# Attention and two gated layers on one core: value matmuls of two steps back to back, and both ends of the run in halves

## What is computed

```python
def attn(x, ...):                      # 16 heads of 8 features
    q, k, v = split((x @ w_qkv).reshape(B, S, 16, 24))
    w = relu(q @ k.T / sqrt(8))
    a = (w / (w.sum(-1) + 1e-6)) @ v
    return layernorm(x + a @ w_out + b_out) * gamma + beta

def ffn(x, ...):                       # w1, w2 dequantised from integers
    h = layernorm(x) * ln_gamma + ln_beta
    return x + 0.5 * (silu(h @ w1 + b1) @ w2 + b2)

x = x + 0.5 * ffn(layernorm(x))
x = x + attn(layernorm(x))
x = x + 0.5 * ffn(layernorm(x))
```

## Time and profile before

| | us |
|---|---|
| median of 3 runs | 387.11 (385.79 to 387.66) |
| the profiled execution, in all | 389.17 |
| its span, first to last instruction | 387.4 |
| TensorE busy | 376.3 (97%) |
| VectorE busy | 285.6 (74%) |
| ScalarE busy | 224.9 (58%) |
| GpSimd busy | 219.4 (57%) |

### The profile page before, as it was taken

How to read it: one execution, slowest core, us unless ns; L and a number is a source line. 1 busy time by engine, 2 the same in 40 slices (tenths; PEclk the granted TensorE clock), 3 DMA queues, 4 the chain that set the end, 5 groups by cost and what they waited for, 6 DMA issues and landing times.

```text
span 387.4 us, 11728 instructions
## 1 busy us (share of the span) xinstructions
PE 376.3 (97%) x4614; PEld 195.3 (50%) x4614; DVE 285.6 (74%) x682; ACT 224.9 (58%) x406; POOL 219.4 (57%) x446
## 2 busy tenths in 40 slices
PE   8988999999999999999999999999999999999996
PEld 8863523353564435553454445553564445323685
DVE  3544687889767988688877977787867977876660
ACT  2235556666756577466857577566756675646302
POOL 4685035737891589438982589437973574263052
PEclk9998999999999999999999999999999999989999
DMA  7318101710171006400261006400350016200001
GB/s 141 50 34 186 30 1 43 177 29 3 32 188 57 3 3 145 104 28 2 57 164 58 2 3 151 122 2 2 83 139 30 2 26 148 73 3 2 3 13 45
DMA packets 14967, 23.05 MB, mean 60 GB/s; under 512 B 3136, under 2 KB 4416, under 8 KB 14912
## 3 DMA queue, kind: packets, MB, share of 16 engines
q1 hardware_dynamic: 11520, 17.71, 19.4%
q10 hardware_dynamic: 3392, 4.59, 4.7%
HBM read 3.41 MB, written 2.10 MB: 14 GB/s over the span
## 4 chain that ended last, share of the span: by engine, by line
PE 80%; DVE 6%; DMA 5%; POOL 3%; issue 2%; ACT 1%; SPq 1%; ACTq 0%; POOLq 0%; DVEq 0%
PE o_bank L439 29%; PE scores L424 15%; PE post_bank L369 9%; PE pre_bank L369 8%; PE pre_bank L374 5%; DMA q_op<-q_parts 3%; PE pre_bank L375 3%; DMA b_rows<-in_L_ffn_fc_bias_dram 2%; PE post_bank L374 2%; DVE probs L815 2%; PE pre_bank L362 2%; PE pre_bank L399 2%; PE post_bank L399 2%; PE post_bank L375 2%; PE post_bank L362 1%
## 5 line engine op out<-in xcount | busy, mean ns | idle before, releaser
L815 DVE TENSOR_SCALAR probs<-scores 128x512 f32<-128x512 f32 x256 | 164.0, 682 | 50.5 <-PE scores L424 48.1
L608 ACT ACTIVATE probs<-scores 128x512 f32<-128x512 f32 x256 | 138.6, 595 | 69.4 <-PE scores L424 69.2
L439 PE MATMUL o_bank<-probs,v_op 128*32 128x512 f32 x1024 | 137.9, 611 | 0.0
L424 PE MATMUL scores<-q_op,k_op 32*128 32x512 f32 x512 | 78.4, 498 | 2.6 <-DMA q_op<-q_parts 2.0
L424 PEld LDWEIGHTS scores<-q_op,k_op 32*128 32x128 f32 x512 | 32.0, 183 | 87.9 <-issue 51.6
L439 PEld LDWEIGHTS o_bank<-probs,v_op 128*32 128x32 f32 x1024 | 21.7, 109 | 30.4 <-issue 24.9
L540 ACT ACTIVATE pre_y<-pre_bank,b_sum,s_col 128x512 f32<-128x512 f32 x28 | 21.8, 779 | 25.8 <-PE pre_bank L399 25.8
L844 POOL TENSOR_SCALAR norm_x_var<-norm_x_mv 128x4 f32<-128x4 f32 x24 | 4.7, 196 | 53.1 <-DVE norm_x_mv L678 52.6
L844 POOL TENSOR_SCALAR norm_y_var<-norm_y_mv 128x4 f32<-128x4 f32 x8 | 1.7, 218 | 55.2 <-DVE norm_y_mv L678 55.2
L369 PE MATMUL pre_bank<-w,pre_y 128*32 128x128 f32 x1024 | 32.3, 274 | 0.0
L369 PEld LDWEIGHTS pre_bank<-w,pre_y 128*32 128x32 f32 x1024 | 27.3, 110 | 8.0 <-issue 8.0
(11 more groups left out here) (133 smaller groups left out, 534.6 us busy)
## 6 DMA issues: line engine op xcount, KB each, us to landing
k_op<-k_parts SPq DMA_DIRECT2D x64, 128.0 KB, 2.7
q_op<-q_parts SPq DMA_DIRECT2D x63, 128.0 KB, 2.8
pre_x<-in_L_attn_x_dram ACTq DMA_DIRECT2D x8, 256.0 KB, 2.8
out_dram<-o_rows ACTq DMA_DIRECT2D x8, 256.0 KB, 2.0
w_int<-in_L_ffn_fc_q_dram SPq DMA_DIRECT2D x2, 256.0 KB, 3.9
s_rows<-in_L_ffn_fc_scales_dram SPq DMA_DIRECT2D x1, 256.0 KB, 6.9
w_raw<-in_L_attn_w_qkv_dram SPq DMA_DIRECT2D x1, 192.0 KB, 7.8
wo<-in_L_attn_w_out_dram SPq DMA_DIRECT2D x8, 8.0 KB, 7.4
```

The lines of the kernel that those rows point to most:

```text
L424: mm(scores[i][:, j, :], k_op[rows, g, P * kt:P * (kt + 1)], q_op[rows, g, :], start=True, stop=True).then_inc(scores_done[i], 1)
L439: last = mm(o_bank[pair][VW * j:VW * (j + 1), :], v_op[:, kt, heads_of(g).start + 2 * j, :], probs[:, s % 2, j, :], start=(odd == 0 and kt ...
L608: activation(probs[:, s % 2, j, :], scores[0][:, j, :], ACT.Relu).then_inc(probs_done[0], 1)
L815: v.tensor_scalar(probs[:, s % 2, 2 + j, :], scores[1][:, j, :], 0.0, None, ALU.max).then_inc(probs_done[1], 1)
```

## The change

- Values are issued in even steps only: those of s-2 and s-1, one after the other, behind the scores of s. `probs` gets a third buffer, taken in turn over the whole run (`HELD`), and the evictions wait for the values of three steps ago.
- *pre* of batch 0 and *post* of batch 7 are worked in two halves of 256 tokens (`first.*`, `last.*`, function `edge` on TensorE, ScalarE and VectorE, `half_deviations` on GpSimd). The halves take the banks of both stages and separate semaphores; q and k of batch 0 take score banks, halves of `op` the `pre` bank and `o_bank[0]`. Batch 0's `x` is loaded in two halves by two queues, the last result stored in two.
- Small constants come in two arrays: four columns in one, four rows (b2, gamma, beta, b_out) in another, each loaded by one DMA; the host lays them side by side. `b2_quarter` is made inside the first residual, behind the mix. 
- `alone`, `bank` and the special cases for it are gone. All orders are new.

The core of the diff:

```diff
+HELD = 3
...
 PE_FIRST = [
-    "warm_up.19", "pre.hT", "weights.b1", "warm_up.2", "pre.fc1.0", "pre.fc1.1", "pre.fc1.2", "pre.fc1.3", "pre.fc2.0", "pre.fc2.1",
-    "pre.fc2.2", "pre.fc2.3", "warm_up.15", "pre.uT", "warm_up.3", "pre.k", "pre.q", "pre.v", "warm_up.7", "pre.hT@1", "warm_up.4"
+    "warm_up.14", "weights.b1", "warm_up.2", "first.hT.0", "first.fc1.0.0", "first.fc1.1.0", "first.fc1.2.0", "first.hT.1",
+    "first.fc1.3.0", "first.fc2.0.0", "first.fc1.0.1", "first.fc2.1.0", "first.fc2.2.0", "first.fc2.3.0",
+    "first.fc1.1.1", "first.fc1.2.1", "first.fc1.3.1", "first.fc2.0.1", "first.fc2.1.1", "first.fc2.2.1",
+    "first.fc2.3.1", "warm_up.9", "first.uT.0", "first.k.0", "first.q.0", "first.uT.1", "first.v.0", "first.k.1",
+    "first.q.1", "first.v.1", "warm_up.4", "pre.hT@1", "warm_up.5"
 ]
 PE_ORDER = [
-    ([], ["post.fc2.0@-2", "pre.fc1.0@1"]),
-    (["post.fc2.1@-2", "post.fc2.2@-2", "post.fc2.3@-2", "pre.fc1.1@1"], []),
-    (["post.op@-1", "pre.fc1.2@1"], []),
+    ([], ["post.fc1.3@-2", "pre.fc1.0@1"]),
+    (["post.fc2.0@-2", "pre.fc1.1@1", "post.fc2.1@-2", "post.fc2.2@-2", "post.fc2.3@-2"], []),
+    (["pre.fc1.2@1", "post.op@-1"], []),
     (["pre.fc1.3@1"], []),
-    (["pre.fc2.0@1"], []),
-    ([], ["pre.fc2.1@1"]),
+    ([], []),
+    (["pre.fc2.0@1", "pre.fc2.1@1"], []),
+    ([], []),
     (["pre.fc2.2@1", "pre.fc2.3@1"], []),
     ([], []),
+    (["post.hT@-1"], []),
     ([], []),
-    ([], ["post.hT@-1"]),
-    ([], []),
-    ([], ["pre.uT@1", "post.fc1.0@-1"]),
-    ([], ["pre.k@1", "post.fc1.1@-1"]),
-    ([], ["pre.q@1", "post.fc1.2@-1"]),
+    (["post.fc1.0@-1", "pre.uT@1"], []),
+    ([], ["pre.k@1"]),
+    (["post.fc1.1@-1", "pre.q@1"], []),
     ([], ["pre.v@1"]),
-    (["post.fc1.3@-1", "pre.hT@2"], []),
+    (["post.fc1.2@-1", "pre.hT@2"], []),
 ]
 PE_LAST = ([], [
-    "post.fc2.0@-2", "post.fc2.1@-2", "post.fc2.2@-2", "post.fc2.3@-2", "post.op@-1", "warm_up.32@-1", "post.hT@-1", "warm_up.5@-1",
-    "post.fc1.0@-1", "post.fc1.1@-1", "post.fc1.2@-1", "post.fc1.3@-1", "post.fc2.0@-1", "post.fc2.1@-1",
-    "post.fc2.2@-1", "post.fc2.3@-1"
+    "post.fc1.3@-2", "post.fc2.0@-2", "last.op.0@-1", "last.op.1@-1", "post.fc2.1@-2", "post.fc2.2@-2",
+    "post.fc2.3@-2", "warm_up.26@-1", "last.hT.0@-1", "last.fc1.0.0@-1", "last.fc1.1.0@-1", "last.fc1.2.0@-1", "last.hT.1@-1",
+    "last.fc1.3.0@-1", "last.fc2.0.0@-1", "last.fc1.0.1@-1", "last.fc1.1.1@-1", "last.fc1.2.1@-1",
+    "last.fc1.3.1@-1", "last.fc2.0.1@-1", "last.fc2.1.1@-1", "last.fc2.2.1@-1", "last.fc2.1.0@-1",
+    "last.fc2.2.0@-1", "last.fc2.3.0@-1", "last.fc2.3.1@-1"
 ])
 ACT_FIRST = [
-    "pre.hT", "pre.fc1.0", "pre.fc1.1", "pre.load_x", "pre.fc1.2", "pre.fc1.3", "pre.load_x@1", "pre.uT",
-    "pre.k", "pre.q", "pre.v", "pre.hT@1"
+    "first.hT.0", "first.fc1.0.0", "first.hT.1", "first.fc1.1.0", "first.fc1.2.0", "first.fc1.3.0",
+    "first.fc1.0.1", "pre.load_x@1", "first.fc1.1.1", "first.fc1.2.1", "first.fc1.3.1", "first.uT.0",
+    "first.t_u.0", "first.k.0", "first.q.0", "first.uT.1", "first.t_u.1", "first.k.1", "first.v.0",
+    "first.q.1", "pre.load_x", "first.v.1", "pre.hT@1"
 ]
 ACT_ORDER = [
-    ["pre.fc1.0@1"],
+    ["post.fc1.3@-2", "pre.fc1.0@1"],
     ["pre.fc1.1@1"],
-    ["pre.fc1.2@1", "post.store@-2", "pre.load_x@2"],
+    ["pre.load_x@2", "pre.fc1.2@1"],
     ["pre.fc1.3@1"],
     ["post.y_apply@-1"],
     [],
     [],
     [],
     [],
+    [],
     ["post.hT@-1"],
-    [],
     ["pre.uT@1", "post.fc1.0@-1"],
-    ["pre.k@1", "post.fc1.1@-1"],
-    ["pre.q@1", "post.fc1.2@-1"],
-    ["pre.v@1"],
-    ["pre.hT@2", "post.fc1.3@-1"],
+    ["pre.k@1"],
+    ["pre.q@1"],
+    ["post.fc1.1@-1", "pre.v@1"],
+    ["post.store@-2", "post.fc1.2@-1", "pre.hT@2"],
 ]
 ACT_LAST = [
-    "post.hT@-1", "post.store@-2", "post.fc1.0@-1", "post.fc1.1@-1", "post.fc1.2@-1", "post.fc1.3@-1",
-    "post.store@-1"
+    "post.fc1.3@-2", "last.hT.0@-1", "last.fc1.0.0@-1", "post.store@-2", "last.fc1.1.0@-1", "last.hT.1@-1",
+    "last.fc1.2.0@-1", "last.fc1.3.0@-1", "last.fc1.0.1@-1", "last.fc1.1.1@-1", "last.fc1.2.1@-1",
+    "last.fc1.3.1@-1", "last.store.0@-1", "last.store.1@-1"
 ]
 DVE_FIRST = [
-    "pre.x_stats", "pre.x_apply", "weights.w1", "weights.w1_parts", "pre.hT", "weights.b1", "weights.w2",
-    "weights.w_qkv", "pre.x1", "pre.x1_stats", "pre.x_stats@1", "pre.u_apply", "pre.uT", "pre.k_lo",
-    "pre.q_lo", "pre.hT@1"
+    "first.x_stats.0", "first.x_stats.1", "weights.w1", "first.x_apply.0", "weights.w1_hi", "weights.w1_lo",
+    "weights.b1", "first.hT.0", "first.x_apply.1", "weights.w2", "first.hT.1", "weights.w_qkv", "first.x1.0",
+    "first.x1_stats.0", "first.u_apply.0", "pre.x_stats@1", "first.x1.1", "first.uT.0", "first.x1_stats.1",
+    "first.k_lo.0", "first.u_apply.1", "first.q_lo.0", "first.uT.1", "first.k_lo.1", "first.q_lo.1", "pre.hT@1"
 ]
 DVE_ORDER = [
     ["oT.1@-1", "den.1@-1"],
-    ["a.1@-1", "post.out@-2", "aT@-1"],
+    ["a.1@-1", "aT@-1", "post.out@-2"],
     ["post.y@-1", "post.y_stats@-1"],
     [],
     ["pre.x_stats@2"],
     ["post.x2@-1"],
-    ["post.x2_stats@-1", "pre.x1@1"],
-    [],
+    ["post.x2_stats@-1"],
+    ["pre.x1@1"],
     ["pre.x1_stats@1"],
     [],
     ["post.hT@-1"],
-    [],
-    ["oT.0", "den.0", "pre.k_lo@1"],
+    ["oT.0"],
+    ["den.0", "pre.k_lo@1"],
     ["pre.q_lo@1"],
     ["a.0"],
     ["pre.hT@2"],
 ]
 DVE_LAST = [
-    "oT.1@-1", "den.1@-1", "a.1@-1", "aT@-1", "post.out@-2", "post.y@-1", "post.y_stats@-1", "post.y_apply@-1",
-    "post.x2@-1", "post.x2_stats@-1", "post.x_apply@-1", "post.hT@-1", "post.out@-1"
+    "oT.1@-1", "den.1@-1", "a.1@-1", "aT@-1", "last.y.0@-1", "last.y.1@-1", "last.y_stats.0@-1",
+    "last.y_apply.0@-1", "last.y_stats.1@-1", "last.x2.0@-1", "last.y_apply.1@-1", "last.x2_stats.0@-1",
+    "last.x2.1@-1", "post.out@-2", "last.x_apply.0@-1", "last.x2_stats.1@-1", "last.hT.0@-1",
+    "last.x_apply.1@-1", "last.hT.1@-1", "last.out.0@-1", "last.out.1@-1"
 ]
 POOL_FIRST = [
-    "pre.x_stats", "weights.b2", "pre.xr", "pre.x1_stats", "pre.x_stats@1", "pre.x_apply@1", "pre.xr@1",
-    "v_in.0", "post.u_bias", "pre.uT", "v_in.1", "pre.x1_beta"
+    "first.x_stats.0", "first.x_stats.1", "pre.xr", "first.x1_stats.0", "first.x1_stats.1", "pre.x_stats@1",
+    "pre.x_apply@1", "v_in.0", "pre.xr@1", "pre.x1_beta", "v_in.1", "pre.uT", "post.u_bias"
 ]
 POOL_ORDER = [
     [],
     [],
-    ["post.y_stats@-1", "post.y_gamma@-1"],
-    [],
-    ["v_in.2", "post.x2_stats@-1", "post.x_apply@-1", "pre.x1_stats@1"],
-    [],
+    [],
+    [],
+    ["v_in.2", "v_in.3", "post.y_gamma@-1", "pre.x_stats@2"],
+    [],
+    ["post.x2_stats@-1", "post.x_apply@-1"],
+    [],
+    ["pre.x1_stats@1"],
     ["pre.u_apply@1"],
-    ["pre.x_stats@2", "pre.uT@1"],
-    [],
-    ["v_in.3", "pre.x_apply@2", "post.xr@-1"],
-    [],
-    ["v_in.0@1", "v_in.1@1"],
-    ["pre.x1_beta@1"],
-    [],
-    ["post.u_bias@1", "pre.xr@2"],
+    [],
+    ["pre.uT@1", "post.u_bias@1", "pre.x_apply@2", "pre.x1_beta@1", "post.xr@-1"],
+    ["v_in.0@1"],
+    ["pre.xr@2"],
+    ["v_in.1@1", "post.y_stats"],
     [],
 ]
 POOL_LAST = [
-    "post.y_stats@-1", "post.x2_stats@-1", "post.x_apply@-1", "post.xr@-1", "post.y_gamma@-1"
+    "last.y_stats.0@-1", "post.x2_stats@-1", "last.y_stats.1@-1", "last.x2_stats.0@-1", "last.x2_stats.1@-1",
+    "post.xr@-1", "post.y_gamma@-1"
 ]
...
-        probs = sb("probs", [P, 2, HG, S])
+        probs = sb("probs", [P, HELD, HG, S])
...
+            sp.dma_start(pre.x[:, rows_in(1), :], x_rows[0][:, rows_in(1), :]).then_inc(x_loaded, 16)
             for dst, src, loaded in (
-                (w1_int[:, :], fc1_q, w1_loaded), (s1_col[:, :], fc1_scales.rearrange("(p f) -> p f", f=FT), s1_loaded),
+                (w1_int[:, :], fc1_q, w1_loaded),
                 (w2_int[:, :, :], fc2_q.rearrange("(g p) n -> p g n", p=P), w2_loaded),
...
-                              probs[:, s % 2, j, :], start=(odd == 0 and kt == 0), stop=(odd == 1 and kt == TT - 1))
+                              probs[:, (STEPS * b + s) % HELD, j, :], start=(odd == 0 and kt == 0), stop=(odd == 1 and kt == TT - 1))
...
-                    if s > 0:
-                        step_values(b, s - 1)
-                    elif b > 0:
-                        step_values(b - 1, STEPS - 1)
+                    if s % 2 == 0:
+                        for n in range(STEPS * b + s - 2, STEPS * b + s):
+                            if n >= 0:
+                                step_values(*divmod(n, STEPS))
...
+            for s in range(STEPS - 2, STEPS):
+                step_values(B - 1, s)
...
+            act.dma_start(pre.x[:, rows_in(0), :], x_rows[0][:, rows_in(0), :]).then_inc(x_loaded_a, 16)
+            act.dma_start(col_consts[:, :], columns.rearrange("(p n) -> p n", p=P)).then_inc(cols_loaded, 16)
+            act.dma_start(rows4[:, :, :], lines.unsqueeze(0).to_broadcast([P, 4, D])).then_inc(rows_loaded, 16)
...
-                    if STEPS * b + s - 1 > 0:
```

(20 more changed lines are left out.)

443 lines of the change are left out of this document (290 added, 153 removed).

## The result

| | before | after |
|---|---|---|
| median of 4 runs | 387.38 us (385.79 to 388.21) | 398.06 us (397.06 to 399.38) |
| span of the profiled execution | 387.4 | 397.6 |
| mean granted clock of its TensorE | 0.991 | 0.983 |

The ratio is 1.0283, with a 95% interval of 1.0237 to 1.0329: the change makes the kernel 10.7 us slower. The profiled execution took 399.38 us in all, 1.3 above the median. The other three have a mean clock of 0.991, this one 0.983, so it probably holds a fall of the clock that they don't.

The account below looks back on a forecast made before the run. TensorE's in-order queue, plus scores waiting for evictions, was taken as the bound. From a 387.4 us span, -1.4 + 0.8 + 7.8 + 2.8 - 4.0 = +6.0 gave 393.4; on the median the forecast was 393.0, range 382 to 401.

Parts of the forecast that it names:

- The chain of 2.41: Full batches: value pairs start 2.41 us after the odd step's scores, held by evictions; waits sum to 2.15 per batch.
- my list of work: Full batch: TensorE's new queue priced item by item for s0 to s15, in all 40.97 us without waits.
- s8, VectorE late: Full batches: work in VectorE's queue pushes eviction 7, adding 0.13 us before s8.
- s12 and s13, k's low part: Full batches: k's low part lands between the scores and the eviction of s13 on VectorE, about 0.7 us.
- s15 and s0, queries' DMA: Batch boundary: a 0.23 us pair wait from s15, plus 0.24 because the queries' DMA holds the next batch's first scores.
- Rival 1: Layout holds but VectorE's queue doesn't matter: +0.16 per full batch, 384.0 us in all; chance 0.16.
- rival 2: Waiting scores hide in the pairs, only saved work counts: 0.87 less per full batch, 376.5 us; chance 0.12.
- The same layout, with s9 empty: Batch 0: without post work, s9 waits 1.55 us; batch takes 38.6 to 40 instead of 38.19, +0.8.
- rival 3: Clock falls inside full batches too, up to 1.9 us each: +7 to +11, 400 to 404 us; chance 0.14.
- My 1.9 for a fall: Batch 7: two value groups in a row at the half clock take 1.9 us more, part of +2.8.
- Laying both halves out: End: with the last stage worked in halves, the last store is issued at about 381 instead of 384.93, -4.0 us.
- the statistic in VectorE's queue: Start: pre.x_stats@1 waits for a load ahead of x1.1, putting it at about 18.3; the start gains only 1.4 us.

Follow-up runs that it names:

- the last experiment: Changed kernel with VectorE's row statistic pre.x1_stats@1 issued in s9, behind eviction 9, instead of in s8: 407.39 us, ratio 1.0511.
- filled: Changed kernel with identity matmuls in s1, s3, s9, s11 of batch 0, and 12 instead of 5 ahead of its first scores: 395.87 us, ratio 1.0208.
- the tuned pairs: Changed kernel, pairs kept, with 3 and 16 identity matmuls instead of 9 and 26 at the ends, and fillers in batch 0: 392.47 us, ratio 1.0152.
- Singles: Changed kernel with single values and the old full-batch orders, 3 and 16 identity matmuls at the ends, fillers in batch 0: 383.2 us, ratio 0.9887.
- the ends alone: Changed kernel with single values, two probabilities buffers and the old full-batch orders, keeping halved ends and joined constants: 387.54 us, ratio 0.9989.

## Why the prediction was right or wrong

The forecast was 393.0 with a range of 382 to 401; 398.06 lies in it, on the side that I called likeliest, but above the 388.5 to 397 that I gave 0.52. The forecast is 5 us short, and the table of stages says of which terms: batch 0 by 3.0, the end by 2.9 and the start by 1.3 too low, the full batches by 1.7 and batch 7 by 1.3 too high. That the errors cancel in part is luck.

**Right: the waits of the pairs.** The chain of 2.41 from the odd S to the V pair is there to the hundredth (170.44 to 172.85). Batch 3 step by step, the excess over my list of work:

| step | forecast wait | measured |
|---|---|---|
| s4 (from s3) | 0.66 | 0.64 |
| s9 and s10 | 1.03 + 0.25 | 1.20 |
| s12 (from s11) | 0.23 | 0.20 |
| s8, VectorE late | 0.13 | 0 |
| s12 and s13, k's low part | 0.7 | 0.42 in s13 |
| s14 | 0 | 0.29 |
| s15 and s0, queries' DMA | 0.23 + 0.24 | 0 in batch 3 (0.4 to 0.7 in batches 2, 4 and 6) |

The six full batches came to +6.1 against +7.8, with +1.18 for each of batches 2 to 6 against +1.3. The sizes that I was unsure of, k's low part above all, were somewhat high, and batch 1 came to +0.22 because its waits in s0 are covered when batch 0 is slow. The 0.42 of s13 stays with short evictions and the 0.29 of s14 goes; that k's low part makes the one I argued, and no run took it away. Rival 1 falls by the size, +1.18 against +0.16, and by the 0.18 of s9, which the last experiment took away; rival 2 falls by the 2.41. What I didn't weigh is the orders: single values in the same orders wait more still (44.86 a batch), so the waits can't be put down to the pairs as such.

**Wrong: batch 0, +3.8 against +0.8.** The step that failed is "The same layout, with s9 empty": it counted waits and no clock. I looked for a fall in batch 7, where the kernel before has one, and not in the batch without post work to which the new layout adds waits. The kernel before has one here too, so "The trace agrees at 345 us only" (rival 3) was a misreading, and the 38.19 that I compared with holds it. First a window of before, then the same of before with short evictions, whose batch 0 has full ones:

```profile
33.00:36.00 3.00, 3.00 (x13) 0.87 (x12) 1.16 (x2) 1.98 (x4) 1.02 (x2) 0.60 0.87 241
```

```profile
33.00:36.00 3.00, 3.00 (x21) 0.99 (x23) 1.35 (x3) 2.23 (x5) 0.48 (x2) 1.00 0.83 202
```

With the clock at 1.00 throughout, the old batch 0 takes 36.38 and the new one 38.25 (filled) or 38.93 (in the last experiment, unfilled, with its statistic moved). So without the clock the new batch 0 costs 1.9 to 2.5, not 0.8, the falls of after add 3.1 to 3.8, and the fall of before hides 1.8. In after, value pairs of 3.29 and 3.11 stand where 1.92 was priced. Batches 0 and 1 together took 82.35 in after and 79.76 in the tuned pairs, so over both batches, since batch 1 gives a part back, the falls are worth about 2.6 in this trace, and less in the median, as its other executions had a higher clock. Rival 3 named the mechanism, but for the full batches, and none of them had it in after; the kernel with one pair parted had one in batch 1, the one with the statistic of s8 moved in batch 6.

**Wrong: batch 7, +1.5 against +2.8.** My 1.9 for a fall was not due. Its S wait as long as those of batch 0, and yet the clock is 1.00 throughout:

```profile
346.62 1.14 PE L448 MATMUL scores<-q_op,k_op 32*128 32x512 f32 x4 [0.82 <-ACT probs L724]
...
350.79 1.24 PE L448 MATMUL scores<-q_op,k_op 32*128 32x512 f32 x4 [0.74 <-ACT probs L724]
...
346.60:350.80 4.20, 3.44 (x25) 1.23 (x25) 2.52 (x6) 3.64 (x9) 2.59 (x6) 1.00 0.00 0
```

Two errors cancelled in part. The layout's end was near (39.63 laid out, 40.26 measured). But the 38.74 of before, to which I compared it, holds the fall of the earlier trace rows. Singles without a fall there take 37.27, so the pairs with their orders really cost 3.0 in this batch, more than twice what they cost in a full one.

**Wrong: the end, -1.1 against -4.0.** The step that failed is "Laying both halves out": I laid out VectorE, ScalarE and the matmuls of the work, and left the 52 identity matmuls of `warm_up.26` out of TensorE's queue, though the diff shows them. They take 6.07 us and end 2.3 after the rows that stand behind them are ready. Cutting them to 32 gave 2.2 of the missing 2.9 back. The other 0.7 stays open: in after the last fc2 products run from 391.5 to 394.2, and I did not try their order.

**Wrong in part: the start, -0.13 against -1.4.** GpSimd's residual came early as forecast (14.05), and x1.1 ran at 18.37 (18.3 forecast). But the second half of q_lo ended at 26.52, not 25.4. The step that failed is the clock once more, which the lengths of steps took as full: it is 0.83 in 21 to 24 and 0.60 in 24 to 27. Two kernels with the same nine identity matmuls and no fall here, the ends alone and the filled one, have the first S at 29.97 and 30.00, and in the ends alone q_lo ends at 25.58. So the fall is 0.9 of the missing 1.3. That the layout holds so well without it is luck in part: uT.0 stood behind `warm_up.9` for 1.7 us, which I had not laid out either, and with `warm_up.3` the first S is at 28.93, although the clock falls there too. The reason that I gave, the statistic in VectorE's queue, delays x1.1 by about 1 us, but moving it made the start later, not earlier.

So the errors were terms left out of a queue that the diff shows (2.3 at the end, 1.7 at the start), and the clock: left out in batch 0 and in the start, put into batch 7 where it didn't fall, and overlooked in the batches of before that I compared with.

## What to carry to other kernels

With one set of score banks, the start of one score group to the end of the next is set by the eviction (2.47 us here), so moving the value groups about only moves the wait. What counts is how the other work is spread: a pair wants 1.55 us of it in its odd step, single values want it in every step (an S behind an empty step waited 0.5). When a change comes with new orders, run the old rule in the new orders as well; here that was the run which parted the two. Price the keep-busy matmuls of an order like any other work: they run to their end, whether what stands behind them is ready or not. Where a change adds waits, ask of each stage by itself what the clock will do, and whether the stage of before that it is compared with holds a fall.

## What the runs showed of the hardware

- The half clock came in batch 0 and not in batch 7, though the scores wait alike in both, and in batch 0 the number of falls differs between kernels whose full batches are the same (42.01 in after, 39.56 with one pair parted). A fall also came in a start (21 to 27 us in after, none in the ends alone with the same start). What sets it stays open.
- With identity matmuls in four steps of batch 0 (the six of s9, twelve in the trace, took 1.60 us) the clock stayed at 1.00 there in both traces that have them with pairs. It stayed at 1.00 in one trace without them, too.
- VectorE's evictions of 0.75 instead of 1.29 us brought the time from the start of one S to the end of the next from 2.48 to 1.94.
- A statistic issued one step later on VectorE (186.12 instead of 183.57) cost TensorE 1.64 us two steps on.
- Halving an instruction's columns doesn't halve its time: VectorE's sum takes 0.41 for 256 columns against 0.69 for 512, GpSimd's power 0.71 for 128x2 against 1.01 for 128x4.
